# A transformer layer on one core: the first norm one section further ahead, the residual's input loaded a second time

## The chip, the core and the metric

The program runs on one core of one Trainium2 chip. A core has a matrix engine (TensorE, PE in the profile; its weight loads are PEld), a vector engine (VectorE, DVE), a scalar engine (ScalarE, ACT), a general engine (GpSimd, POOL) and a synchronising engine (SyncE, SP) that here issues nearly all DMA transfers. Each engine runs its own list of instructions in order, and they wait for each other on semaphores. The metric is the device time of one execution in microseconds, smaller is better.

## What is computed

One pre-norm layer on 4 sequences of 1024 tokens with 256 features: latent attention with 16 heads, then a mixture of 16 experts of which each token takes 2, beside a shared dense expert. Cut to what matters:

```python
h = layernorm(x)
q = (h @ Wqa @ Wqb)                      # 16 heads, 64 plain + 64 rotary columns
ckv, k_pe = split(h @ Wkva, 64)          # latent keys/values, rotary key
k, v = split(ckv @ Wkvb); rope(q_pe, k_pe)
x = x + softmax(causal(q @ k.T / sqrt(128))) @ v @ Wo     # the residual
h2 = layernorm(x)
top2 = top_k(softmax(h2 @ gate.T), 2)
out = x + sum_over_top2(w * swiglu(h2, expert)) + swiglu(h2, shared)
```

## The kernel before, in words

The 4096 tokens are 32 tiles of 128 rows. The program has a start (weights are multiplied together, scaled and split into pairs of 16-bit numbers), 32 attention sections with two more to drain them, then the experts' rows and the final sum. A batch is one sequence, 8 tiles, so 8 sections; section t is section t % 8 of its batch. A tile attends to all tiles before it in its batch, so sections grow: 2 units of heads in the first, 4 in the second, 8 in the third and fourth, 16 from the fifth on.

Section t does the attention of tile t, and beside it the side work of other tiles, at fixed places (unit k, place sub) from the tables `FIRST_TILE`, `SECOND`, `MIDDLE`, `LONG`, which all engines read. The side work, by tile:

- tile t+3: its first norm. VectorE makes mean and variance (`means`), GpSimd the rest (`norm`): 14 small steps for the inverse root, then xn, and the pair xs of 16-bit halves. SyncE turns xs into xT (`turn_x`), in one of two buffers.
- tile t+2: its projections by TensorE from xT into the one side bank of PSUM (`lat`, `pe0`, `pe1`, `q0`, `q1`). ScalarE and VectorE copy them out as high and low halves: the latent into `ks_sb`, the queries into `qs`, which lies in the tile `work` (`query_hi`, `query_lo`). Rotary columns go through GpSimd (`rope`). SyncE then turns the keys (`turn_keys`, ks_sb into kT) and the queries (`turn_queries`, work into qT). `query_hi` of a tile waits until the queries' transpose of the tile before has landed, since it overwrites what that one reads: `act.wait_ge(s.qT_in, 16 * n)`.
- tile t-1: the second half of the attention's output is normed, split and turned into oT (`turn_output`), TensorE multiplies it by the output weights (`out`), VectorE adds the input and writes x1 (`residual`). `means` and `norm` then take x1 of tile t-1 and the x of tile t+3 in one go, the x1 part first; SyncE turns both (`turn_x2`, `turn_x`).
- tile t-2: router and dense expert (`gate`, `up`, the hidden row turned by `turn_hidden`, `down`), and the rows are scattered to the experts' lists.

The input tiles stand in `x_sb`, five buffers, from the load until the residual has read them. So `load_x(m)` waits for the residual of tile m-5.

`section` of SyncE sets the order of all transposes, loads and stores in one queue, and a wait in it holds all that stands behind. `side` of TensorE puts the first projection that reads xT (`lat`) at (0, 3) in the second section of a batch, at (0, 1) in the third and fourth, at (0, 2) in the later ones.

## Time and profile before

| | us |
|---|---|
| runs (3), median | 1942.01 |
| lowest, highest | 1939.42, 1942.53 |
| profiled execution, its own time | 1940.04 |
| its span | 1938.2 |
| busy: PE, DVE, ACT, POOL | 1567.4, 1309.4, 1030.4, 978.7 |
| DMA moved | 139.76 MB, mean 72 GB/s |

The mean granted clock of TensorE is 0.924 of full speed. The span runs from the first instruction to the last end; the execution's own time has 1.8 us around it. An engine's busy time says how much it works, not whether the end waits for it. That is what the chain says: it is followed back from the last instruction, at each step to what released it. The list of waits counts every idle stretch that a wait ended, on the chain or off it.

### The profile page before, as it was taken

The page shows a single profiled execution, that of the slowest core. Times are in us where ns is not written, and L with a number is a line of the kernel's source. Part 1 is how long each engine was busy: PE and PEld are TensorE (multiplying, and loading weights), DVE is VectorE, ACT ScalarE, POOL GpSimd, SP SyncE. Part 2 cuts the span into 40 slices and gives each one's busy share as a digit, 9 for nine tenths or more (in the row PEclk, how much of TensorE's full clock was granted, in tenths as well). Part 3 has the DMA queues.
Part 4 walks back from the last instruction along what each step waited for, and adds up shares of the span by engine and source line. Part 5 has one row for each costly group of instructions (what it writes and reads, how often), then busy time and mean ns, then how long its engine had stood idle before and what let it go on. Part 6 is the DMA issues. An engine that isn't in the chain of part 4 may idle for free.

```text
span 1938.2 us, 45912 instructions
## 1 busy us (share of the span) xinstructions
PE 1567.4 (81%) x16418; PEld 1111.6 (57%) x16419; DVE 1309.4 (68%) x2960; ACT 1030.4 (53%) x2344; POOL 978.7 (50%) x1570
## 2 busy tenths in 40 slices
PE   8555779999868899997788999968889997379990
PEld 3133556766646667666466666655666765256660
DVE  1445877788766677887576787867667886245556
ACT  1323556666545666665455666645556663156660
POOL 2023656755566666644676664646566334134340
PEclk9667899999989999999899999989999999599995
DMA  5056333212234322213422323133322211543327
GB/s 151 0 153 120 55 60 71 60 31 46 58 63 88 65 57 53 44 25 59 93 60 56 56 56 54 30 67 72 64 55 50 51 23 31 124 138 104 102 81 260
DMA packets 329045, 139.76 MB, mean 72 GB/s; under 512 B 276656, under 2 KB 323795, under 8 KB 328790
## 3 DMA queue, kind: packets, MB, share of 16 engines
q1 hardware_dynamic: 313942, 113.14, 28.4%
q0 software_dynamic: 6912, 16.83, 2.7%
q10 hardware_dynamic: 8000, 7.23, 1.3%
q8 instruction: 123, 2.02, 0.4%
q14 instruction: 68, 0.56, 0.1%
HBM read 42.58 MB, written 29.53 MB: 37 GB/s over the span
## 4 chain that ended last, share of the span: by engine, by line
PE 50%; DVE 19%; ACT 7%; DMA 7%; issue 6%; POOL 6%; SPq 3%; DVEq 1%; ACTq 0%; POOLq 0%
PE of_ps L576 23%; PE s_ps L576 15%; PE t_ps L732 10%; DVE pT L1437 5%; DVE smax L1408 3%; ACT pT L885 2%; POOL xn L562 2%; DMA wd_sb<-wd 1%; ACT probs L1009 1%; DVE smax L1412 1%; DVE nmax L1416 1%; SPq L406 1%; ACT work L885 1%; DMA xT<-xs 1%; POOL xs L566 1%
## 5 line engine op out<-in xcount | busy, mean ns | idle before, releaser
L1437 DVE TENSOR_TENSOR pT<-t_ps,pT 128x512 f16<-128x512 f32 (+3 forms) x688 | 409.9, 598 | 188.7 <-ACT pT L885 186.6
L576 PE MATMUL s_ps<-kT,qT 128*128 128x512 f16 (+3 forms) x2304 | 498.9, 331 | 18.0 <-DMA qT<-work 14.1
L885 ACT CAST pT<-t_ps 128x512 f16<-128x512 f32 (+3 forms) x688 | 354.5, 515 | 271.4 <-PE t_ps L732 271.3
L732 PE MATMUL t_ps<-id,probs 128*128 128x128 f32 x2304 | 388.6, 284 | 67.6 <-ACT probs L1009 31.8
L732 PEld LDWEIGHTS t_ps<-id,probs 128*128 128x128 f32 x2304 | 262.6, 144 | 170.2 <-issue 84.8
L576 PE MATMUL of_ps<-weights,xT 128*128 128x512 f16 (+1 forms) x960 | 231.8, 385 | 136.6 <-DMA xT<-xs 87.7
L576 PEld LDWEIGHTS s_ps<-kT,qT 128*128 128x128 f16 x2304 | 221.0, 100 | 88.1 <-DMA qT<-work 14.3
L1009 ACT ACTIVATE probs<-s_ps,nmax,fac 128x640 f32<-128x640 f32 (+3 forms) x256 | 269.1, 1051 | 1.1 <-DVE nmax L1416 1.0
L576 PEld LDWEIGHTS of_ps<-ckv,pT 128*128 128x128 f16 x6912 | 244.4, 99 | 43.2 <-DVE o_sb L1278 10.4
L576 PE MATMUL of_ps<-ckv,pT 128*128 128x64 f16 x6912 | 261.2, 194 | 8.0 <-DVE o_sb L1278 7.7
L576 PEld LDWEIGHTS of_ps<-weights,xT 128*128 128x128 f16 x960 | 88.7, 108 | 230.6 <-issue 118.6
L1625 POOL TENSOR_TENSOR os_<-o_sb,os_ 128x512 f16<-128x512 f32 x64 | 74.7, 1167 | 224.6 <-ACT os_ L885 216.1
L1408 DVE TENSOR_REDUCE smax<-s_ps 128x1 f32<-128x512 f32 (+1 forms) x256 | 157.4, 648 | 3.9 <-PE s_ps L576 3.7
L1713 POOL DMA_INDIRECT y_exp<-probs,work x80 | 78.7, 984 | 149.3 <-ACT probs L1098 143.2
L1609 POOL TENSOR_TENSOR work<-work,sin_sb 128x544 f32<-128x544 f32 x64 | 102.0, 1594 | 96.8 <-ACT work L885 68.0
L885 ACT COPY work<-of_ps 128x512 f32<-128x512 f32 (+1 forms) x96 | 44.6, 464 | 199.3 <-PE of_ps L576 197.3
L1014 ACT ACTIVATE probs<-s_ps,nmax,fac 128x256 f32<-128x256 f32 (+3 forms) x224 | 144.1, 649 | 1.1 <-DVE nmax L1419 1.1
L1390 DVE TENSOR_REDUCE smax<-s_ps 128x1 f32<-128x768 f32 (+2 forms) x136 | 122.8, 903 | 13.0 <-PE s_ps L576 12.2
L576 PE MATMUL s_ps<-maskbf,idbf 128*128 128x128 bf16 x512 | 114.5, 224 | 0.0
L1412 DVE TENSOR_REDUCE smax<-s_ps 128x1 f32<-128x512 f32 (+2 forms) x160 | 95.4, 627 | 21.6 <-PE s_ps L576 21.3
L576 PE MATMUL of_ps<-weights,oT 128*128 128x256 f16 x768 | 90.7, 276 | 8.8 <-DMA oT<-os_ 6.0
L576 PEld LDWEIGHTS of_ps<-weights,oT 128*128 128x128 f16 x768 | 74.4, 99 | 21.6 <-ACT work L885 5.1
(201 smaller groups left out, 2448.5 us busy)
## 6 DMA issues: line engine op xcount, KB each, us to landing
work<-lists SPq DMA_DIRECT2D x80, 128.5 KB
wgu_sb<-wgu SPq DMA_DIRECT2D x2, 2816.0 KB, 14.9
x_sb<-x SPq DMA_DIRECT2D x32, 128.0 KB, 2.4
dense<-den SPq DMA_DIRECT2D x32, 128.0 KB
weights<-dense SPq DMA_DIRECT2D x1, 4096.0 KB, 17.9
qT<-y_exp SPq DMA_DIRECT2D x16, 256.0 KB, 5.8
work<-y_exp SPq DMA_DIRECT2D x16, 256.0 KB, 7.6
layer_out<-weights ACTq DMA_DIRECT2D x16, 256.0 KB, 5.7
```

Of the source, the lines that this page charges most:

```text
L576: return pe_.matmul(o, a, b, start=start, stop=stop)
L732: last = pe_.transpose(t_ps[:, h, c * P:(c + 1) * P], probs[:, u % 2, g * L + j * P:g * L + (j + 1) * P], id32[:, :])
L885: return act.copy(o, i)
L1009: act.activation(probs[:, par, 0:L], s_flat[:, 1024 * par:1024 * par + L], ACT.Exp, bias=nmax[:, par, 0:1], scale=f_att, accum_out=ssum[:, ...
L1014: last = act.activation(probs[:, par, g * L:(g + 1) * L], s_flat[:, base:base + L], ACT.Exp, bias=nmax[:, par, g:g + 1], scale=f_att, accu ...
L1390: dve.tensor_reduce(smax[:, par, 0:G], view, AX_X, ALU.max).then_inc(s.maxs, 1)
L1408: last = dve.tensor_reduce(smax[:, par, h:h + 1], bank[:, 0:(j1 - j0) * P], AX_X, ALU.max)
L1412: last = dve.tensor_reduce(smax[:, par, h * n:(h + 1) * n], view, AX_X, ALU.max)
L1437: dve.tensor_tensor(pT[:, u % 2, 1, h, 0:w], t_ps[:, h, 0:w], pT[:, u % 2, 0, h, 0:w], ALU.subtract).then_inc(s.lo_p, 1)
L1609: st_.do(pool.tensor_tensor(rot2[:, :, k:ROPE:2], pe[:, :, 1 - k:ROPE:2], sin_b, ALU.mult))
L1625: pool.tensor_tensor(os_[:, 1, :], o_sb[:, :], os_[:, 0, :], ALU.subtract).then_inc(s.lo_o, 1)
L1713: pool.indirect_dma_start(y_exp, bass.IndirectOffsetOnAxis(xg[:, q, 2 * D:ROW].bitcast(I32), 0), m_ys[:, q % YB, :], None, bounds_check=NY ...
```

## The change

The first norm is made one section further ahead: section t norms tile t+4 together with x1 of tile t-1. xT gets a third buffer, and so does `ks_sb`. The start makes three norms before the weights' scales instead of two. An input tile is done with once its norm is made, so `x_sb` has two buffers; for the residual the tile is loaded a second time (`load_residual`), straight into the x1 buffer in which the sum is then made in place. On SyncE, `load_x` now stands at the head of a section and waits for a norm of the section before; `load_residual` stands in front of the transpose of the second half of the attention's output.

```diff
--- before.py
+++ after.py
@@ -51,7 +51,8 @@
 UPRE = [sum(UNITS[:i]) for i in range(TB)]
 LN_STEPS = 14
 NEWTON = 3
-XS = 5
+XS = 2
+KS = 3
 SPLIT_MAX = [g > 1 or i >= 6 for i, g in enumerate(GROUP)]
 
 
@@ -184,13 +185,13 @@
         ln_w = sb("ln_w", [P, 3, 2], F32)
         xn = sb("xn", [P, D], F32)
         xs = sb("xs", [P, 2 * D], F16)
-        xT = sb("xT", [P, 2, 2, KD, P], F16)
+        xT = sb("xT", [P, 3, 2, KD, P], F16)
         NPE = (H + 1) * ROPE
         work = sb("work", [P, 2 * NPE + H * HD + HD], F32)
         pe = work[:, 0:NPE].rearrange("p (h r) -> p h r", r=ROPE)
         rot2 = work[:, NPE:2 * NPE].rearrange("p (h r) -> p h r", r=ROPE)
         qs = work[:, 2 * NPE:2 * NPE + H * HD].bitcast(F16).rearrange("p (s h d) -> p s h d", s=2, h=H)
-        ks_sb = sb("ks_sb", [P, 2, 2, HD], F16)
+        ks_sb = sb("ks_sb", [P, KS, 2, HD], F16)
         qT = sb("qT", [P, 2, 2, H * P], F16)
         kT = sb("kT", [P, 2, S], F16)
         ckv = sb("ckv", [P, 2, TB, C], F16)
@@ -245,7 +246,8 @@
         s = namedtuple("Signals", names)(*(sem(n) for n in names))
 
         xin = [sem(f"x_in{k}") for k in range(XS)]
-        k_in = [sem(f"keys_in{k}") for k in range(2)]
+        k_in = [sem(f"keys_in{k}") for k in range(KS)]
+        x1_in = [sem(f"x1_in{k}") for k in range(2)]
         xn_s = [sem(f"xn_made{k}") for k in range(2)]
         scattered = [sem(f"scattered{k}") for k in range(2)]
         stored = [sem(f"stored{k}") for k in range(2)]
@@ -337,7 +339,7 @@
         t_row, t_exp = t_tab[:, 0:1], t_tab[:, 1:2]
         tab = sb("tab", [1, 2, NMT], I32)
         free_i = sb("free_i", [1, E], I32)
-        pad = x_sb[:, 2:4, :].rearrange("p a n -> p (a n)").bitcast(F16)[:, 0:ROW]
+        pad = x_sb[:, 0:2, :].rearrange("p a n -> p (a n)").bitcast(F16)[:, 0:ROW]
         w_s, w_t = xn[:, 0:NT], xn[:, NT:2 * NT]
         w_k = xn[:, 2 * NT:4 * NT].rearrange("p (t k) -> p t k", k=TOPK)
 
@@ -366,7 +368,7 @@
             load(r_wqaT[0:QLB, 1, :], wqaT[P:QL, :], s.w_a)
             load(r_pe[:, 0, :], wqb_peT[0:P, :], s.w_a)
             load(r_pe[0:QLB, 1, :], wqb_peT[P:QL, :], s.w_a)
-            for k in range(3):
+            for k in range(XS):
                 load(x_sb[:, k, :], x[k * P:(k + 1) * P, :], xin[k])
             load(r_wvT, wvT, s.w_o)
             load(r_wo, wo.rearrange("(h d) n -> d h n", d=VD), s.w_o)
@@ -378,16 +380,21 @@
 
             def load_x(m):
 
-                if has(m - XS):
-                    sp.wait_ge(s.side_free, JOB["out", m - XS] + 1)
+                sp.wait_ge(s.ln1_done, 2 * (m - XS + 1))
                 sp.dma_start(x_sb[:, m % XS, :], x[m * P:(m + 1) * P, :]).then_inc(xin[m % XS], 16)
+
+            def load_residual(p):
+                if has(p - 2):
+
+                    sp.wait_ge(s.dense_done, p - 1)
+                sp.dma_start(x1[:, p % 2, :], x[p * P:(p + 1) * P, :]).then_inc(x1_in[p % 2], 16)
 
             def turn_x(m):
                 sp.wait_ge(s.ln1_done, 2 * (m + 1))
-                if has(m - 2):
-
-                    sp.wait_ge(s.side_made, JOB["q1", m - 2] + 1)
-                sp.dma_start_transpose(xT[:, m % 2].rearrange("p a k n -> p (a k) n"), xs[:, :]).then_inc(s.xT_in, 16)
+                if has(m - 3):
+
+                    sp.wait_ge(s.side_made, JOB["q1", m - 3] + 1)
+                sp.dma_start_transpose(xT[:, m % 3].rearrange("p a k n -> p (a k) n"), xs[:, :]).then_inc(s.xT_in, 16)
 
             def turn_x2(p):
                 sp.wait_ge(s.ln2_done, 2 * (p + 1))
@@ -413,7 +420,7 @@
 
                     last = n - i - 1
                     sp.wait_ge(s.s_made, 2 * (unit_of(last, units(last) - 1) + 1))
-                sp.dma_start_transpose(kT[:, :, i * P:(i + 1) * P], ks_sb[:, n % 2].rearrange("p s d -> p (s d)")).then_inc(k_in[n % 2], 16)
+                sp.dma_start_transpose(kT[:, :, i * P:(i + 1) * P], ks_sb[:, n % KS].rearrange("p s d -> p (s d)")).then_inc(k_in[n % KS], 16)
 
             def turn_output(p, hh):
                 sp.wait_ge(s.lo_o, 2 * p + hh + 1)
@@ -431,18 +438,19 @@
                                        hs[:, :, :].rearrange("p a n -> p (a n)")).then_inc(s.hT_in, 16)
 
             def section(t):
-                n, p, q, m = t + 2, t - 1, t - 2, t + 3
+                n, p, q, m = t + 2, t - 1, t - 2, t + 4
                 i = t % TB if has(t) else None
+                if has(m + 1):
+                    load_x(m + 1)
                 if has(q) and i == 0:
                     turn_hidden(q)
                 if has(p):
+                    load_residual(p)
                     turn_output(p, 1)
                 if has(q) and i not in (0, 1):
                     turn_hidden(q)
                 if i in (0, 2, 3):
                     turn_output(t, 0)
-                if has(m + 1):
-                    load_x(m + 1)
                 if has(p):
                     turn_x2(p)
                 if has(m):
@@ -463,7 +471,10 @@
                     store_dense(q)
 
             turn_x(0)
+            load_x(2)
             turn_x(1)
+            load_x(3)
+            turn_x(2)
             turn_keys(0)
             turn_queries(0)
             section(-1)
@@ -627,7 +638,7 @@
             def project(n, name, c0, w):
                 side_bank(name, n)
                 pe_.wait_ge(s.xT_in, 16 * (n + 1))
-                split_product(f_ps[:, 0:w], lambda a, k: xT[:, n % 2, a, k, :], lambda b, k: wq[:, b, k, c0:c0 + w],
+                split_product(f_ps[:, 0:w], lambda a, k: xT[:, n % 3, a, k, :], lambda b, k: wq[:, b, k, c0:c0 + w],
                               list(range(KD))).then_inc(s.side_made, 1)
 
             def latent(n):
@@ -696,7 +707,7 @@
                 G, par, L = GROUP[i], u % 2, (i + 1) * P
                 if u == 0 and h == 0:
                     pe_.wait_ge(s.qT_in, 16 * (t + 1))
-                    pe_.wait_ge(k_in[t % 2], 16 * (t // 2 + 1))
+                    pe_.wait_ge(k_in[t % KS], 16 * (t // KS + 1))
                 for g, j0, j1 in halves(i)[h]:
                     base = 1024 * par + s_off(i, g)
                     c0, c1 = j0 * P, j1 * P
@@ -926,11 +937,11 @@
                 if n > 0:
 
                     act.wait_ge(s.rope_done, n)
-                if n > 1:
-                    act.wait_ge(k_in[n % 2], 16 * (n // 2))
-                    act.wait_ge(s.ckv_ready, n - 1)
+                if n >= KS:
+                    act.wait_ge(k_in[n % KS], 16 * (n // KS))
+                    act.wait_ge(s.ckv_ready, n - KS + 1)
                 copy(pe[:, H, :], f_ps[:, C:2 * C])
-                copy(ks_sb[:, n % 2, 0, 0:C], f_ps[:, 0:C]).then_inc(s.hi_q, 1)
+                copy(ks_sb[:, n % KS, 0, 0:C], f_ps[:, 0:C]).then_inc(s.hi_q, 1)
 
             def rope_copy(n, g):
                 act.wait_ge(s.side_made, JOB[f"pe{g}", n] + 1)
...
@@ -1237,12 +1248,12 @@
 
             def latent_lo(n):
                 dve.wait_ge(s.hi_q, 3 * n + 1)
-                dve.tensor_tensor(ks_sb[:, n % 2, 1, 0:C], f_ps[:, 0:C], ks_sb[:, n % 2, 0, 0:C], ALU.subtract).then_inc(s.side_free, 1)
+                dve.tensor_tensor(ks_sb[:, n % KS, 1, 0:C], f_ps[:, 0:C], ks_sb[:, n % KS, 0, 0:C], ALU.subtract).then_inc(s.side_free, 1)
 
             def latent_copy(n):
 
                 dve.wait_ge(s.side_free, JOB["lat", n] + 1)
-                dve.scalar_tensor_tensor(ckv[:, :, n % TB, :], ks_sb[:, n % 2, :, 0:C], 1.0, ks_sb[:, n % 2, :, 0:C], ALU.mult,
+                dve.scalar_tensor_tensor(ckv[:, :, n % TB, :], ks_sb[:, n % KS, :, 0:C], 1.0, ks_sb[:, n % KS, :, 0:C], ALU.mult,
                                          ALU.max).then_inc(s.ckv_ready, 1)
...
@@ -1280,7 +1291,8 @@
 
             def residual(p):
                 dve.wait_ge(s.side_made, JOB["out", p] + 1)
-                dve.scalar_tensor_tensor(x1[:, p % 2, :], f_ps[:, 0:D], f_out, x_sb[:, p % XS, :],
+                dve.wait_ge(x1_in[p % 2], 16 * (p // 2 + 1))
+                dve.scalar_tensor_tensor(x1[:, p % 2, :], f_ps[:, 0:D], f_out, x1[:, p % 2, :],
                                          ALU.mult, ALU.add).then_inc(s.side_free, 1)
 
             def means(n, p):
@@ -1375,9 +1387,9 @@
                     out_norm(t, 0)
                 if due("out", p, t, k, sub):
                     residual(p)
-                    means(t + 3, p)
+                    means(t + 4, p)
                 if t == 0 and (k, sub) == (1, 3):
-                    means(3, -1)
+                    means(4, -1)
                 if due("down", q, t, k, sub):
                     places(q)
 
@@ -1446,6 +1458,7 @@
 
             means(0, -1)
             means(1, -1)
+            means(2, -1)
             first_weights()
             other_weights()
             latent_lo(0)
@@ -1455,7 +1468,7 @@
             rope_sum(0)
             rope_lo(0)
             lo_parts(FIRST, FIRST + 1)
-            means(2, -1)
+            means(3, -1)
             latent_lo(1)
             latent_copy(1)
             lo_parts(FIRST + 1, len(SPLITS))
...
@@ -1660,6 +1673,7 @@
 
             norm(pool, 0, -1)
             norm(pool, 1, -1)
+            norm(pool, 2, -1)
             pool.wait_ge(s.amax_ready, 1)
             pool.partition_all_reduce(amax_all[:, 0:2], amax[:, 0:2], P, bass.bass_isa.ReduceOp.max).then_inc(s.amax_reduced, 1)
             pool.wait_ge(s.amax_ready, 2)
@@ -1681,7 +1695,7 @@
                 if i in (0, 2, 3):
                     out_lo(t, 0)
                 if t < NT:
-                    norm(pool, t + 3, p)
+                    norm(pool, t + 4, p)
                 if i == 1:
                     if has(q):
                         hidden_lo(q)
```

SyncE's queue from the end of the first section of a batch (section 8) to the transposes of section 9, with the semaphores waited for. Before (lines: 416 keys, 406 queries, 377 dense store, 423 attention's output oT, 383 load of x, 397 and 390 the two norms, 430 hidden row):

```order
L416 DMA_TRANSPOSE kT<-ks_sb 128x2x128 [waits rope_done]
L406 DMA_TRANSPOSE qT<-work 128x32x128 [waits s_made,side_free,rope_done]
L377 DMA dense<-den 128x256 [waits dense_done]
L423 DMA_TRANSPOSE oT<-os_ 128x8x128 [waits side_made,lo_o]
L383 DMA x_sb<-x 128x256 [waits side_free]
L397 DMA_TRANSPOSE x2T<-xs 128x4x128 [waits side_made,ln2_done]
L390 DMA_TRANSPOSE xT<-xs 128x4x128 [waits side_made,ln1_done]
L430 DMA_TRANSPOSE hT<-hs 128x6x128 [waits side_made,lo_h]
L423 DMA_TRANSPOSE oT<-os_ 128x8x128 [waits side_made,lo_o]
```

and now (423 keys, 413 queries, 379 dense store, 384 load of x, 390 load of the residual's input, 430 oT, 404 and 397 the two norms, 437 hidden row):

```order
L423 DMA_TRANSPOSE kT<-ks_sb 128x2x128 [waits rope_done]
L413 DMA_TRANSPOSE qT<-work 128x32x128 [waits s_made,side_free,rope_done]
L379 DMA dense<-den 128x256 [waits dense_done]
L384 DMA x_sb<-x 128x256 [waits ln1_done]
L390 DMA x<-x 128x256 [waits dense_done]
L430 DMA_TRANSPOSE oT<-os_ 128x8x128 [waits side_made,lo_o]
L404 DMA_TRANSPOSE x2T<-xs 128x4x128 [waits side_made,ln2_done]
L397 DMA_TRANSPOSE xT<-xs 128x4x128 [waits side_made,ln1_done]
L437 DMA_TRANSPOSE hT<-hs 128x6x128 [waits side_made,lo_h]
L430 DMA_TRANSPOSE oT<-os_ 128x8x128 [waits side_made,lo_o]
```

The load of x has moved from behind oT to in front of it, and the new load stands there too.

SyncE's queue at the start, from the first transposed input to the first weights of the experts. Before:

```order
L390 DMA_TRANSPOSE xT<-xs 128x4x128 [waits ln1_done] x2
L416 DMA_TRANSPOSE kT<-ks_sb 128x2x128 [waits rope_done]
L406 DMA_TRANSPOSE qT<-work 128x32x128 [waits side_free,rope_done]
L383 DMA x_sb<-x 128x256
L390 DMA_TRANSPOSE xT<-xs 128x4x128 [waits side_made,ln1_done]
L416 DMA_TRANSPOSE kT<-ks_sb 128x2x128 [waits rope_done]
L406 DMA_TRANSPOSE qT<-work 128x32x128 [waits side_free,rope_done]
L360 DMA wgu_sb<-wgu 128x16x352 [waits lo_made]
```

and now:

```order
L397 DMA_TRANSPOSE xT<-xs 128x4x128 [waits ln1_done]
L384 DMA x_sb<-x 128x256 [waits ln1_done]
L397 DMA_TRANSPOSE xT<-xs 128x4x128 [waits ln1_done]
L384 DMA x_sb<-x 128x256 [waits ln1_done]
L397 DMA_TRANSPOSE xT<-xs 128x4x128 [waits ln1_done]
L423 DMA_TRANSPOSE kT<-ks_sb 128x2x128 [waits rope_done]
L413 DMA_TRANSPOSE qT<-work 128x32x128 [waits side_free,rope_done]
L384 DMA x_sb<-x 128x256 [waits ln1_done]
L397 DMA_TRANSPOSE xT<-xs 128x4x128 [waits side_made,ln1_done]
L423 DMA_TRANSPOSE kT<-ks_sb 128x2x128 [waits rope_done]
L413 DMA_TRANSPOSE qT<-work 128x32x128 [waits side_free,rope_done]
```

Each load of x now waits for a norm, a third xT stands ahead of the first keys, and the fourth (tile 3) ahead of the second keys; behind it the experts' weights come as before.

## Rows read from the trace of the kernel before

**Rows 1.** The page, part 4: shares of the chain that ended last, by engine.
```profile
...
PE 50%; DVE 19%; ACT 7%; DMA 7%; issue 6%; POOL 6%; SPq 3%; DVEq 1%; ACTq 0%; POOLq 0%
...
```

**Rows 2.** The list of waits: us in total, times, longest us.
```profile
...
PE of_ps L576 <- DMA xT<-xs: 87.7, 13, 18.5
...
```

**Rows 3.** TensorE in order of time: start, us, instruction [idle before <-releaser].
```profile
...
171.49 0.80 PE L576 MATMUL of_ps<-weights,xT 128*128 128x128 f16 x6 [18.52 <-DMA xT<-xs]
173.58 1.09 PE L732 MATMUL t_ps<-id,probs 128*128 128x128 f32 x4 [1.30 <-DVE pT L1437]
...
552.41 0.80 PE L576 MATMUL of_ps<-weights,xT 128*128 128x128 f16 x6 [9.96 <-DMA xT<-xs]
...
623.19 0.80 PE L576 MATMUL of_ps<-weights,xT 128*128 128x128 f16 x6 [4.87 <-DMA xT<-xs]
...
665.10 0.80 PE L576 MATMUL of_ps<-weights,xT 128*128 128x128 f16 x6 [4.67 <-DMA xT<-xs]
...
```

**Rows 4.** The chain in order of time, 545 to 590 us: start, us, what.
```profile
...
552.43 6.14 SPq L406
...
558.63 0.58 SPq L377
...
559.30 3.21 DMA oT<-os_
...
578.39 2.80 DMA hT<-hs
...
```

**Rows 5.** SyncE in order of time, a plain load of x.
```profile
...
541.13 0.58 SPq L383 DMA_DIRECT2D x_sb<-x  x1
```

**Rows 6.** Stretches: us, busy (x) of PE, PEld, DVE, ACT, POOL, then granted clock.
```profile
...
552.00:556.00 4.00, 3.59 (x20) 2.80 (x21) 1.32 (x4) 1.30 (x4) 1.96 (x3) 0.50 0.87 87
623.00:627.00 4.00, 3.81 (x19) 2.43 (x20) 1.82 (x5) 1.57 (x5) 1.46 (x2) 0.60 0.88 170
665.00:669.00 4.00, 3.90 (x35) 2.66 (x36) 1.41 (x4) 0.33 (x2) 1.38 (x2) 0.50 0.98 102
...
```

**Rows 7.** TensorE in order of time: out and down projections, sections 9, 32.
```profile
...
562.65 2.78 PE L576 MATMUL of_ps<-weights,oT 128*128 128x256 f16 x24 [1.35 <-DMA oT<-os_]
...
581.24 1.54 PE L576 MATMUL of_ps<-weights,hT 128*128 128x256 f16 x9 [1.49 <-DMA hT<-hs]
...
1635.85 4.45 PE L576 MATMUL of_ps<-weights,oT 128*128 128x256 f16 x24 [2.23 <-DMA oT<-os_]
...
```

**Rows 8.** The chain in order of time, 600 to 672 us.
```profile
...
620.63 2.42 DMA xT<-xs
...
662.55 2.41 DMA xT<-xs
...
```

**Rows 9.** SyncE in order of time: queries' transposes in sections 11, 12, 27.
```profile
...
623.21 5.22 SPq L406 DMA_TRANSPOSE qT<-work  x1
...
665.14 6.22 SPq L406 DMA_TRANSPOSE qT<-work  x1
...
1374.14 6.13 SPq L406 DMA_TRANSPOSE qT<-work  x1
...
```

**Rows 10.** DMA issues, the same three: median us from issue to landing.
```profile
...
qT<-work SPq DMA_TRANSPOSE x1, 7.7
...
qT<-work SPq DMA_TRANSPOSE x1, 7.9
...
qT<-work SPq DMA_TRANSPOSE x1, 8.9
```

**Rows 11.** ScalarE in order of time: first queries' copy, the same sections.
```profile
...
633.35 0.58 ACT L885 CAST work<-of_ps 128x512 f16<-128x512 f32 x1 [0.74 <-PE of_ps L576]
...
676.16 0.59 ACT L885 CAST work<-of_ps 128x512 f16<-128x512 f32 x1 [0.60 <-PE of_ps L576]
...
1384.29 0.59 ACT L885 CAST work<-of_ps 128x512 f16<-128x512 f32 x1 [0.74 <-PE of_ps L576]
...
```

**Rows 12.** GpSimd in order of time, 19 to 90 us.
```profile
...
59.44 0.38 POOL L1664 PARTITION_ALL_REDUCE amax_all<-amax  x1 [26.83 <-DVEq L1188]
...
```

More of the change, by code:

```diff
@@ L1501, in _ @@
             residual(NT - 1)
-            means(NT + 3, NT - 1)
+            means(NT + 4, NT - 1)
             places(NT - 2)
-            norm(dve, NT + 3, NT - 1)
+            norm(dve, NT + 4, NT - 1)
             gate_hidden(NT - 1)
```

8 lines of the change are left out of this document (4 added, 4 removed).

## The prediction

> **What bounds the kernel now.** I read the chain that ended last first. Half of it is TensorE, a fifth VectorE, and only 7% DMA and 6% GpSimd [rows 1]. The change goes after one wait. The list of waits says that TensorE's projections stood 13 times for the transposed input xT, 87.7 us in all [rows 2]. That is 4.5% of the span, and the first thing to settle is how much of it the end of the kernel feels. So I went to TensorE's own rows for each of the 13. They repeat by batch of eight sections: about 10.0 us in the second section of a batch, 4.9 and 4.7 in the fourth and fifth [rows 3]. The first batch has its own pair besides, 18.5 us in section 1 and a short one in section 2. By kind: one of 18.5, three of 10.0 (sections 9, 17, 25), eight of 4.4 to 4.9 (sections 3, 4, 11, 12, 19, 20, 27, 28), one short. For each kind I asked the chain whether it runs through that wait, and then what TensorE meets next once it is gone.
>
> **The change part by part.** The norm of tile t+4 instead of t+3 is made in section t. GpSimd makes as many norms, of the same size, at the same places; its order and its durations per section stay. xT of a tile is then needed a whole section later, 40 to 60 us, so all 13 waits should go. What each is worth:
>
> *Section 1, 18.5 us.* After this wait TensorE does 0.8 us of projection and stands again, for VectorE, until 173.58 [rows 3]. VectorE is held there by the search over the expert weights, whose load is issued from the same queue as before. TensorE will only reach 173.58 earlier. Worth 0. The short one in section 2 is followed in the same way by a wait for VectorE; I price it at 0.
>
> *Sections 9, 17, 25, 10.0 us each.* The chain does not run through this wait. It runs along SyncE's queue: keys, then the queries' transpose that takes the queue 6.14 us, the dense store, the transpose of the attention's output (oT) with 3.21 us to its landing, and then the out projection [rows 4]. That projection feeds the residual, the norm, the transpose of the hidden row and the down projection that closes the section [rows 4]. TensorE ahead of time meets oT at the same 562.5 and just waits longer before the out projection. The gain is 0. There is a cost. Two loads (the next x, and the new one of the residual) now stand between the dense store and this oT, where before there was none. One such issue is 0.58 us of SyncE [rows 5], two 1.2. Their 256 KB also go ahead of oT: between 0 and 1 us more, I take 0.3. And TensorE, with its earlier work (about 7 us at full clock) done 10 us sooner, stands some 12 to 14 us before the out projection instead of 1.35, and begins it at half clock. After the 10 us idle of before it ran at 0.50 [rows 6]. The same 24 matmuls took 4.45 us where the clock was low and 2.78 here [rows 7]: 1.7 us more, on the chain. Sum 3.2. Against it, the later chain leaves TensorE less idle before the down projection, which in the old trace starts slow (1.54 us for 9 matmuls) [rows 7]; I give back 0.3. So 2.9 per section, from 1.2 (issues alone) to 5, and 3 x 2.9 = 8.7 us lost.
> The Trainium skill, "DMA: Bandwidth & Descriptors", section "Queues, rings and completion order", says that SyncE's transfers share its own row of rings and that each DMA engine takes their descriptors in ring order. It speaks against the change at this place: by it the data of the two loads precede oT's, which is the upper end for that term (1 instead of 0.3); the trace shows the chain along this queue but no plain load ahead of an oT.
>
> *The eight waits of 4.4 to 4.9 us.* Here the chain does run through the wait, with the landing of xT 2.4 us after its issue [rows 8]. What is next late? ScalarE's copy of the query projection into the staging tile first waits until the transpose of the tile before has landed, since that transpose reads the same tile. That transpose is issued right behind xT: at 623.21, 7.7 us to its landing, so 630.9; the copy ran at 633.35. In section 12: 665.14 + 7.9 = 673.0, copy at 676.16. In section 27: 1374.14 + 8.9 = 1383.0, copy at 1384.29 [rows 9 to 11]. So the copy can move forward by 2.4, 3.1 and 1.3 us and no more. The other five, read the same way, average 2.7; all eight together 20 us. What stands queued behind this copy on ScalarE are the exponentials of the next unit and the copies of the turned probabilities, and TensorE waits for these. TensorE without the xT wait would be ready 4.9 us earlier, and 1.6 us more because the slow clock after that wait (0.60 over 4 us, in section 12 0.50) [rows 6] is gone too. So it arrives 6.5 us early and stands about 4 us for ScalarE. Such a stand may lower the clock again: a stand of 4.7 to 4.9 us did, one of 1.35 did not [rows 3, 6, 7]. If it does, 4 us at half speed cost about 2. I take 0.9 as the mean over the eight, 7 in all. Net of this part 20 - 7 = 13 us, from 20 - 16 = 4 to 20.
> The Trainium skill, "TensorE: Matmul & The Clock Gate", Part 1, says that idle is the low state and that activity releases it. By it the new stands, if long enough, are each paid twice, which is the lower end (4).
>
> *The rest.* The residual's reload is 32 more loads of 128 KB, 4 MB on 139.8. In all sections but those three SyncE has a free stretch for them, since it waits for GpSimd's next output. The wait that the residual gains is on a load issued before oT on the same queue, which is in long before the out projection ends. Third buffers for xT and keys remove dependences that the new order would create, and cost nothing. At the start one more norm, some 6 us of GpSimd, goes into 26.8 us in which GpSimd only waits for the first weights' maxima [rows 12]. VectorE waits for the norm before it, while the matmuls of the weights set the pace. Price 0; if that cover failed, 6 us once.
>
> **Sum.** 0 + 0 - 8.7 + 13 = 4.4 us faster. The profiled execution took 1940.0 us (span 1938.2), so 1935.6 by its own clock. It lies 2 us under the median of the runs, 1942.0, and inside their spread (1939.4 to 1942.5). From the median it is 1937.6. I predict 1937.5. A measurement of this kernel can tell about 0.2% (3.9 us) from no change.
>
> **Rivals.**
> 1. *All comes back.* If ScalarE's copy were not held by the queries, each of the eight would give its wait and the slow clock, 6.5 to 7.5, together 56 us, less 8.7: 1895; with everything in the list of waits 1854. For it: the chain's own rows with xT. Against it: the landings of the queries, 1.3 to 3.1 us under the copies [rows 9 to 11], and the chain of section 9 [rows 4]. Short of that, half of the excess could return where the staging wait is softer than I think: about 1915. Chance 0.15.
> 2. *Slower: SyncE's queue.* The mechanism is the one of sections 9, 17 and 25: two loads ahead of oT, then the out projection at half clock. At its upper price, 5 us, it costs 15; with the clock falling after each of the eight new stands their net is 4, so 1942 + 11 = 1953. It decides from the point where the eight give less than 3 x the loss, that is below 1.1 us each at my middle price of 2.9. For it: the chain along SyncE's rows, and a clock at 0.50 after each long idle. Against it: the copies may move 20 us. Chance 0.25.
> 3. *Nothing.* The same two, about equal (7 to 11 us each way): within 3.9 us of before, 1942. The change does what it says, and the waits only change their names. Chance 0.20.
>
> **How the numbers follow.** My forecast, small gain of 1 to 12 us (1930 to 1941), has 0.40; of that 0.28 lies beyond 0.2% and 0.12 within. Faster: 0.28 + 0.15 = 0.43. Same: 0.12 + 0.20 = 0.32. Slower: 0.25. The likeliest case's own range is 1930 to 1941. For 8 in 10 I reach into rival 1 to 1918, and into rival 2 to 1951.
>
> **What would show it.** In the new profile the wait of the projections for xT is gone or under 5 us. In its place: ScalarE's copies of the queries ended by the DMA of the queries, about 4 us in each of the eight sections; and TensorE's out projection in the second section of batches 2 to 4 ended by oT, some 12 to 14 us each, with a granted clock near 0.5 when it begins. If the copies of the queries do not wait, rival 1 holds. If the out projection of section 9 starts no later behind the issue of the queries' transpose than before (562.65 - 552.43 = 10.2 us), my loss term is wrong. A start of the first attention section later than before would contradict the free norm at the start.

## The result, and the profile after

The changed kernel takes 1943.2 us (median of 17 runs, 1940.8 to 1952.2) against 1939.5 us for the kernel before (17 runs on the same chip, 1935.5 to 1943.8). The ratio is 1.0029, with a 95% interval from 1.0017 to 1.0040: slower by 3.3 to 7.8 us (the two medians lie 3.7 us apart). I had predicted 1937.5 us, a small gain. The profiled execution took 1942.9 us, with a span of 1941.1 us. It lies 2.9 us over that of before.

The wait that the change was made for is gone. In the list of waits of the changed kernel, where the projections' wait for xT stood [rows 2], there are now these two (us in total, times, longest):
```profile
...
PE of_ps L587 <- DMA oT<-os_: 44.8, 4, 14.3
...
ACT work L896 <- DMA qT<-work: 36.2, 9, 6.4
...
```
The chain that ended last has less TensorE and more DMA and issue in it than before [rows 1]:
```profile
...
PE 44%; DVE 19%; DMA 9%; issue 8%; ACT 8%; POOL 7%; SPq 4%; DVEq 1%; ACTq 0%; POOLq 0%
...
```

To see where the time went I took the start of each tile's residual on VectorE from both traces, 32 marks, and subtracted. Sections are numbered as in the prediction; the residual of tile p stands in section p+1. Each line is the change of that difference over the sections named (worked out from the traces, plus is later):
```
start, sections 1 and 2                            -4.1
sections 3, 4                                      -6.2
section 5                                          +5.0
section 9 / 17 / 25                                +3.4 / +3.0 / +2.8
sections 11, 12 / 19, 20 / 27, 28                  -0.2 / -1.9 / -0.4
all other sections together                        +1.2
sum, at the residual of the last tile              +2.6
```

**Section 9.** The chain of the changed kernel in order of time (start, us, what), to be read beside [rows 4]:
```profile
...
547.14 5.20 SPq L413
...
552.39 1.05 SPq L379
...
553.49 0.43 SPq L384
...
553.97 0.46 SPq L390
...
554.53 3.59 DMA oT<-os_
...
558.25 5.29 PE of_ps L587 x24
...
```
and TensorE there, with the stretch of these 24 matmuls (us, busy of PE, PEld, DVE, ACT, POOL, then the granted clock):
```profile
...
558.25 5.28 PE L587 MATMUL of_ps<-weights,oT 128*128 128x256 f16 x24 [14.27 <-DMA oT<-os_]
...
```
```profile
...
558.00:563.20 5.20, 4.95 (x24) 3.45 (x25) 0.00 (x0) 0.00 (x0) 0.00 (x0) 0.50 0.00 0
...
```
The two plain loads (L384, L390) stand ahead of oT, TensorE has stood 14.3 us, and the projection takes 5.3 us at a clock of 0.50 (the lower level, 1.2 GHz) where it took 2.8 [rows 7]. Over the three sections, oT is issued 7.4 us behind the queries' transpose instead of 6.5 (means of three), and the projection takes 5.0 us instead of 2.8. That is 0.9 + 2.2 = 3.1 us, the mean of the three shifts. From oT's issue to the projection's start it takes 3.65 us on average, before 3.67, so against the kernel before no third term is needed.

**Section 11.** ScalarE's first query copy, TensorE behind it, and the issues of SyncE, each in order of time:
```profile
...
631.55 0.58 ACT L896 CAST work<-of_ps 128x512 f16<-128x512 f32 x1 [6.45 <-DMA qT<-work]
...
638.06 0.58 ACT L896 CAST work<-of_ps 128x512 f16<-128x512 f32 x1 [3.36 <-PE of_ps L587]
...
```
```profile
...
632.96 1.12 PE L743 MATMUL t_ps<-id,probs 128*128 128x128 f32 x4 [5.28 <-ACT probs L1025]
...
635.26 2.77 PE L587 MATMUL of_ps<-weights,xT 128*128 128x512 f16 x6
...
```
```profile
...
622.21 6.22 SPq L413 DMA_TRANSPOSE qT<-work  x1
...
```
```profile
...
qT<-work SPq DMA_TRANSPOSE x1, 9.0
...
```
This is the wait that was predicted in xT's place: the copy stands 6.45 us for the queries' landing, TensorE stands 5.28 us for ScalarE, and then runs slowly (6 matmuls of 512 columns in 2.77 us, where the same six take 1.46 at full clock in the trace of e2 below; the clock from 634 to 638 us is 0.50). What was not foreseen is the landing itself: 9.0 us after the issue, not 7.7 [rows 10]. The second copy comes 6.5 us behind the first, before 4.3. So section 11 became 1.9 us longer, not shorter. In section 12 (landing 7.8 us) the copy ran 20.9 us behind the residual of section 11 (673.87), before 24.1 (676.16 [rows 11]), and the section gained 2.2 us.

**Section 5.** GpSimd on the chain (start, us, what), and TensorE behind it, first in the changed kernel and then before:
```profile
...
284.65 5.83 issue
290.48 0.37 POOL amax_all L1715
...
290.93 6.88 issue
297.81 1.15 POOL os_ L1638
...
313.43 4.48 DMA hT<-hs
...
```
```profile
...
317.95 1.93 PE L587 MATMUL of_ps<-weights,hT 128*128 128x256 f16 x9 [3.35 <-DMA hT<-hs]
...
```
```profile
...
324.71 1.14 PE L576 MATMUL of_ps<-weights,hT 128*128 128x256 f16 x9
...
```
GpSimd's one reduction over the partitions for the expert weights blocks it for 13 us, as it did before. TensorE comes out of sections 3 and 4 ahead of time and now waits here for the hidden row, which GpSimd makes 2.7 us later behind the residual than before. Its landing is longer too, 4.5 us instead of 2.8. The down projection starts 11.4 us behind the residual instead of 7.9. In this trace that took 5.0 of the 6.2 us back. How much it takes differs from trace to trace: e4 and e1 below, the first with the same instructions up to here, landed this row in 2.8 us, waited 1.1 and 0.5 us for it, and lost 1.1 and 0.5 us in section 5; e8 landed it in 4.4 us and lost 5.2. Why the landing differs is not shown.

### The profile page after: what moved, and what is told of

Its sections match the earlier page's. It is cut to its first block, busy times and chain, and to the rows that moved or that the text cites. A ratio compares the mean times of both kernels' runs of the same rounds, so it can differ in the third digit from the quotient of the medians.

```text
span 1941.1 us, 45991 instructions
## 1 busy us (share of the span) xinstructions
PE 1561.6 (80%) x16418; PEld 1107.8 (57%) x16419; DVE 1310.0 (67%) x2960; ACT 1028.7 (53%) x2344; POOL 981.1 (51%) x1584
## 4 chain that ended last, share of the span: by engine, by line
PE 44%; DVE 19%; DMA 9%; issue 8%; ACT 8%; POOL 7%; SPq 4%; DVEq 1%; ACTq 0%; POOLq 0%
PE of_ps L587 20%; PE s_ps L587 13%; PE t_ps L743 9%; DVE pT L1449 5%; DMA qT<-work 3%; DVE smax L1420 3%; ACT pT L896 3%; POOL xn L573 2%; DMA wd_sb<-wd 1%; ACT probs L1020 1%; ACT probs L1025 1%; DVE nmax L1428 1%; DVE smax L1424 1%; ACT work L896 1%; SPq L413 1%
## 5 line engine op out<-in xcount | busy, mean ns | idle before, releaser
L587 PE MATMUL of_ps<-weights,xT 128*128 128x512 f16 (+1 forms) x960 | 218.7, 367 | 73.4 <-DVE ks_sb L1251 37.4
L587 PEld LDWEIGHTS of_ps<-weights,xT 128*128 128x128 f16 x960 | 83.7, 102 | 161.7 <-DVE ks_sb L1251 40.8
L587 PE MATMUL of_ps<-weights,oT 128*128 128x256 f16 x768 | 98.0, 289 | 47.6 <-DMA oT<-os_ 44.8
```

Of the source, the lines that this page charges most:

```text
L587: return pe_.matmul(o, a, b, start=start, stop=stop)
```

## Experiments

Each kernel was timed against the kernel before on the same chip; ratios have 95% intervals. "Shift" is the change of a section's length against the kernel before, from the traces. The runs of e1 to e4, e9 and e11 to e13 were made where the kernel before takes 1931 us, 0.4% less than here; in their traces the long sections (6 to 8, 13 to 16 and so on) are 0.3 to 1.1 us shorter for that reason, sections 3 to 5, 11 and 12 and their like in later batches by 0.2 at most, as those of e3 show, in which nothing was changed there; sections 9, 17 and 25 have no unchanged counterpart in these runs.

**Loads behind the output's transpose (e1).**
```
                 if has(p):
-                    load_residual(p)
                     turn_output(p, 1)
+                    load_residual(p)
+                if has(m + 1):
+                    load_x(m + 1)      # was first in the section
```


> The changed kernel with SyncE's two plain loads (next x, residual) issued behind the transpose of the attention's output instead of ahead of it, in every section. Theory (part of what sections 9, 17 and 25 lost is the place of the two loads in SyncE's queue): that transpose is issued 1.1 us earlier there, the out projection begins 1.1 to 1.5 us earlier, and the shift of the residual in these three sections against the kernel before falls from 3.4, 3.0 and 2.9 us to about 1.7; the out projection still runs at half clock. Time 1943.2 - 3 x 1.4 = 1939. Rival A (the whole loss is the clock after a stand of 14 us): the shift stays at 2.9 to 3.4, time 1943. Rival B (the loads' 256 KB cost wherever they stand, since they share the DMA engines): the issue moves but the landing does not, time 1943.

Measured 0.9999 (0.9984 to 1.0014), 0.30% below the changed kernel. SyncE in section 9:
```profile
...
547.69 5.20 SPq L413 DMA_TRANSPOSE qT<-work  x1
552.95 1.02 SPq L379 DMA_DIRECT2D dense<-den  x1
554.05 1.23 SPq L430 DMA_TRANSPOSE oT<-os_  x1
555.34 0.57 SPq L390 DMA_DIRECT2D x<-x  x1
...
```
Shifts 1.6, 1.6, 1.9 as the theory had it. oT is issued 1.0 us earlier behind the queries, and its data arrive 0.4 us sooner after the issue (3.2 against 3.65 us to the projection's start). The projection stays slow (5.0 to 5.3 us). Rival A falls by the shifts, rival B by the data's arrival. The ratio stands for 5.8 us, more than the three sections' 4.2; in this trace section 5 also lost less, so the ratio alone would not price the edit.

**Filler in the stand (e4).**
```
                 side_bank("out", p)
+                if p % TB == 0 and p > 0:
+                    for _ in range(60):
+                        mm(f_ps[:, 0:512], wq[:, 0, 0, 0:P], wq[:, 0, 0, 0:512], True, True)
                 pe_.wait_ge(s.oT_in, 32 * (p + 1))
```


> The changed kernel with 60 matmuls of 128x512 on constant weights into the free bank ahead of the wait for the output's transpose in the second section of batches 2 to 4, 12.8 us of work in a stand of 14.2 us; their result is overwritten. Theory (after the long stand the out projection runs at half clock, 5.3 instead of 2.8 us for 24 matmuls, on the chain): the granted clock stays at 1.0, the out projection takes 2.8 us, time 1943.2 - 3 x 2.5 = 1935.7. Rival A (the slow projection is not on the chain, or what follows absorbs it): matmuls faster, time 1942 to 1943. Rival B (the clock is not kept by such work, or falls elsewhere for it): no faster projection, time 1943 or more.

Measured 1.0009 (0.9997 to 1.0021). The projection of section 9:
```profile
...
555.39 2.79 PE L587 MATMUL of_ps<-weights,oT 128*128 128x256 f16 x24 [0.48 <-DMA oT<-os_]
...
```
All three run at 2.8 us; shifts 1.5, 1.2, 1.4. The clock is worth about 1.7 us each, a little less than the 2.2 of the matmuls. Both rivals fall by the projection's time and the shifts. By the times alone rival A would not: the interval overlaps that of the changed kernel (1.0017 to 1.0040), and the theory's 1935.7 us (0.998) lies below it.

**Both together (e15)**, with 56 matmuls of filler.

> The changed kernel with the loads behind the output's transpose, and 56 matmuls as filler in the stand of 12.8 us before the out projection of sections 9, 17 and 25; nothing done for the eight. Theory (the loss in these three sections is the queue's 1 us plus the clock's 2.2 us and nothing else): the residual's shift there goes from 3.4, 3.0 and 2.9 us to -0.2 to 0.3 against the kernel before; time against the kernel before 1.0029 - 9/1939 = 0.998. Rival (a third cause, as the residual's new wait on its reload, holds it once these two are gone): shift 1 or more, ratio 1.000.

Measured 0.9980 (0.9966 to 0.9994), and shifts of 0.0, 0.2 and 0.4 us. So the loss in sections 9, 17 and 25 is these two terms to within 0.4 us; the residual's wait on its reload is no third one.

**The norm back to tile t+3, reload kept (e3).**
```
-                n, p, q, m = t + 2, t - 1, t - 2, t + 4
+                n, p, q, m = t + 2, t - 1, t - 2, t + 3
-                    norm(pool, t + 4, p)
+                    norm(pool, t + 3, p)
```
The same goes for `means`, and the start makes two norms again.

> The changed kernel with the norm of tile t+3 in section t, as in the kernel before; the residual's reload, its two loads ahead of the output's transpose, two input buffers and three buffers for xT and keys stay. Theory: the 13 waits for xT come back with their old lengths (10.0 and 4.4 to 4.9 us), TensorE stands only some 2.5 us before the out projection of sections 9, 17 and 25 and runs it at full clock, so these lose only the issue term, 1.1 to 1.5 us each: 1939.5 + 4 = 1943.5, and the norm one section ahead is then worth nothing in sum (its gain in the eight is eaten by the clock in the three). Rival A (the reload costs nothing, the norm ahead all of the loss): 1939.5. Rival B (the reload costs more than the queue, by traffic or by the residual's new wait): 1946 or more.

Measured 1.0046 (1.0030 to 1.0062), which is rival B's size, though not by its mechanism. The 13 waits for xT were back (88.0 us). The out projection in section 9:
```profile
...
559.60 4.45 PE L585 MATMUL of_ps<-weights,oT 128*128 128x256 f16 x24 [2.88 <-DMA oT<-os_]
...
```
The loads make oT 1.0 to 1.3 us later, TensorE then stands 2.9, 3.8 and 2.4 us instead of 1.4, 1.5 and 0.9, and that is already enough: the projection takes 4.45, 5.28 and 4.45 us, shifts 2.7, 4.0, 2.8. My theory had full clock after such a stand. One microsecond of queue costs three. The norm ahead is not what loses the time, since with it (the changed kernel, 1.0029) the ratio is if anything lower; the intervals overlap. By these rows and by e1 the loads' place is; the norm back together with the loads behind oT was not run.

**The residual's load issued twice (e8)**, on top of e1, the second time into a spare tile.
```
+                sp.dma_start(spare[:, :], x[p * P:(p + 1) * P, :]).then_inc(spare_in, 16)
```


> The kernel with the loads behind the output's transpose, and each residual load issued twice, the second time into a spare tile that nothing reads: 32 more loads of 128 KB. Theory (a reload costs nothing by its traffic, only by its place ahead of the output's transpose): ratio as with the loads behind, 1.000 (0.9984 to 1.0014 measured). Rival (the traffic of the reload itself costs, by lengthening the landing of the transposes near it): 32 loads more cost what the first 32 did; if these were half of the changed kernel's loss, ratio 1.0015 or more.

Measured 1.0000 (0.9989 to 1.0011): 4 MB more cost nothing to be measured against e1 (0.9999), where about 0.2% could be told. The reload costs by its place, not its traffic.

**Queries first (e2).** SyncE's list of a section ends while TensorE is already in the next one: the queries that it issues last in its sections 10 and 11 are those that ScalarE's copy waits for in sections 11 and 12. So the edit is at i = 2 and 3.
```
                 if i in (0, 2, 3):
                     turn_output(t, 0)
+                if i in (2, 3) and has(n):
+                    turn_keys(n)
+                    turn_queries(n)
                 if has(p):
                     turn_x2(p)
...
-                if has(n):
+                if has(n) and i not in (2, 3):
```


> The changed kernel with the transposes of keys and queries issued ahead of those of x2 and x in the third and fourth section of a batch (i = 2, 3), where the queries stand ready while SyncE waits for GpSimd's norm. Theory (the eight waits for xT became ScalarE's wait for the landing of the queries' transpose, 6.5 and 4.0 us long, plus TensorE at half clock after its stand): the queries are issued about 10 us earlier, the wait of ScalarE's query copy in the eight sections goes, so does TensorE's stand of 5.3 and 2.9 us before the turns, and each gives 4 to 6 us: 1943.2 - 8 x 5 = 1903, at least 1915. Rival A (something else is as late there, as VectorE's low parts or GpSimd): the wait changes its name again, time 1938 to 1943. Rival B (the loss is all in sections 9, 17 and 25): 1943.

Measured 0.9828 (0.9811 to 0.9845): 39 us below the changed kernel. SyncE issues the queries 10 us earlier, while it would have waited for GpSimd's norm, and ScalarE's query copy in section 11 waits for TensorE alone:
```profile
...
608.14 1.89 SPq L423 DMA_TRANSPOSE kT<-ks_sb  x1
610.13 4.84 SPq L413 DMA_TRANSPOSE qT<-work  x1
615.06 1.23 SPq L404 DMA_TRANSPOSE x2T<-xs  x1
617.28 1.20 SPq L397 DMA_TRANSPOSE xT<-xs  x1
...
```
```profile
...
623.50 0.58 ACT L899 CAST work<-of_ps 128x512 f16<-128x512 f32 x1 [0.74 <-PE of_ps L590]
...
```
Sections 11, 12, 19, 20, 27 and 28 are each 6.2 to 6.5 us shorter than before, sections 3 and 4 together 7.4. The first rival of the prediction gave 6.5 to 7.5 each, 56 us for the eight, if the copy were not held; with it freed they give 45. Section 5 lost 4.7 us here too.

**The same order in the kernel before (e7).**

> The kernel before (norm of tile t+3, no reload, five input buffers) with keys and queries ahead of x2 and x in the third and fourth section of a batch. Theory (in the eight sections two things are late at the same place, xT at 13.0 us behind the residual and the landing of the queries at 20.6 to 21.9; removing either alone gives little): the query copy is free, but the projections still wait 4.7 to 4.9 us for xT, which follows GpSimd's norm; the copies stay at 23.2 and 24.1 us behind the residual. Ratio 0.999 to 1.001. Rival (the queries' landing alone was the limit, the norm ahead is not needed): 0.983.

Measured 1.0003 (0.9994 to 1.0011). TensorE in section 11:
```profile
...
622.43 0.80 PE L579 MATMUL of_ps<-weights,xT 128*128 128x128 f16 x6 [4.89 <-DMA xT<-xs]
...
```
Queries first alone: nothing. Norm ahead alone: nothing or a loss. Both: 1.7% below the kernel before. Two things were late at one place, and removing either only shows the other. This and e2 together are what shows the queries' landing as the limit of the eight sections.

**Filler ahead of the new stand (e9).**
```
                 # in turn(t, u, h)
+                if i == 3 and u == 2 and h == 1:
+                    pe_.wait_ge(s.lo_p, 2 * (g_ - 1) + h + 1)
+                    for _ in range(15):
+                        mm(t_ps[:, h, :], wq[:, 0, 0, 0:P], wq[:, 0, 0, 0:512], True, True)
                 pe_.wait_ge(s.exp_done, 2 * g_ + h + 1)
```


> The changed kernel with 15 matmuls of 128x512 on constant weights into the turn's own free bank, ahead of TensorE's wait for ScalarE's exponentials in the fourth section of each batch (sections 3, 11, 19, 27), where TensorE newly stands 3.7 to 5.3 us; 3.2 us of work, overwritten afterwards. Theory (the stand is paid twice there: after it TensorE runs at half clock, and the second query copy comes 5.8 to 6.5 us behind the first instead of 4.3): the distance of the two copies returns to about 4.3 us in sections 11, 19 and 27, each gains 1.5 to 2.2, 5 us in sum (section 3 stands elsewhere): ratio 1.0029 - 0.0025 = 1.0004. Rival (the distance of the copies is set by something else, or the clock falls all the same): 1.0029. If the fillers outlast the stand, each section loses their excess.

Measured 0.9992 (0.9981 to 1.0003). The query copies of section 19:
```profile
...
998.93 0.58 ACT L900 CAST work<-of_ps 128x512 f16<-128x512 f32 x1 [5.28 <-DMA qT<-work]
...
1003.03 0.59 ACT L900 CAST work<-of_ps 128x512 f16<-128x512 f32 x1 [1.02 <-PE of_ps L587]
...
```
4.1 us apart in sections 11, 19 and 27 instead of 5.8 to 6.5. The new stand was indeed paid twice. In section 3, where TensorE has no such stand, the same filler widened the distance from 4.1 to 7.2 us. Section 5 gained here too (its wait for the hidden row did not occur, since section 4 was slower in this run), so the 0.37% is not the filler's alone.

**The reduction later (e12).**
```
-                if t == 3:                      # behind the scatter
+                if t == 4:                      # behind the norm
                     pool.wait_ge(s.gu_amax, 1)
                     pool.partition_all_reduce(amax_all[:, 6:8], ...)
-                    if (t, k) == (4, 2):  expert_scales()
+                    if (t, k) == (4, 12): expert_scales()
```


> The changed kernel with GpSimd's one reduction over all partitions for the expert weights (14 us in which GpSimd does nothing else) moved from ahead of section 4's output part to behind section 4's norm, and VectorE's scales from it to a later unit. Theory (what sections 3 and 4 of the first batch gained, 6.2 us, was lost again in the next one because GpSimd, held by this reduction, had the hidden low part 2.6 us later against TensorE: its transpose landed at 11.3 us behind the residual, and the down projection waited 3.5 us): the residual of tile 4 keeps its 6 to 8 us lead, time 1943.2 - 5 = 1938, ratio 1.000. Rival (the 5 us are not GpSimd's but the transpose's own long landing, 4.5 us, or the reduction now holds something in the next section): ratio 1.002 to 1.004.

Measured 1.0038 (1.0021 to 1.0054). The wait for the hidden row went: the down projection started 7.9 us behind the residual instead of 11.4. But VectorE now stood 3.4 us for the reduction at its new place, and TensorE behind it:
```profile
...
331.68 1.09 PE L743 MATMUL t_ps<-id,probs 128*128 128x128 f32 x4 [4.40 <-DVE pT L1449]
...
```
Section 5 lost 6.1 us. So without GpSimd's lateness there is no such wait; that the 5 us can be had by a better place is not shown, and the rival is what came. The same edit on the candidate below (e13):

> The candidate with the later reduction as well. Theory: 5 us more, ratio 0.9735. Rival: with the reduction later GpSimd is late in the next section instead, ratio 0.976 or more.

Measured 0.9784 (0.9767 to 0.9800): the rival, and not to be told from the candidate without it (e11 below).

**Towards a faster kernel.** e5 is e1 and e2 together.

> The changed kernel with both edits: the two plain loads behind the output's transpose, and keys and queries ahead of x2 and x in the third and fourth section of a batch. Theory (two separate losses at different places): the gains add, 0.30% and 2.0% of the time before: ratio to the kernel before 0.9828 - 0.0030 = 0.980, 1900.5 us where before takes 1939.5. Rival (the loads behind the output's transpose now fall into the time in which the queries are in flight, and the one gain eats the other): ratio 0.983 or more.

Measured 0.9817 (0.9805 to 0.9830). The intervals of this and of e2 overlap, so additivity is not shown by the times; the shifts of sections 9, 17 and 25 are 1.6, 1.6 and 2.1 instead of 2.1, 2.9 and 2.7 in e2.

e10 adds:
```
                         turn_keys(n)
+                    if i == 0:
+                        turn_output(t, 1)       # and not again in the next section
                     turn_queries(n)
```


> The kernel with both edits, and in the first section of a batch the transpose of the attention's second output half (oT) issued between keys and queries instead of behind queries and dense store. Theory (in sections 9, 17 and 25 the chain is SyncE's queue: GpSimd has the output's low part ready 13.7 us before the residual in the changed kernel, and the queries' issue and the dense store stand ahead of oT): oT is issued 4 to 5 us earlier, the out projection starts that much earlier, 3 x 4.5 = 13 us: ratio 0.980 - 0.007 = 0.973. The queries go 4 us later there. Rival A (the later queries or the later dense store are then waited for, the gain is given back): ratio 0.979 to 0.982. Rival B (in the first batch, which has no SyncE queue in the way, the queries' delay costs and the others gain nothing): 0.983 or more.

Measured 0.9814 (0.9801 to 0.9827). Shifts of sections 9, 17, 25: -0.9, -1.1, -0.8, so 2.5 to 2.8 us better each than in e5. Sections 2 and 3 gave back 2.9 us: in the first batch the later queries are waited for (TensorE stood 3.0 us for them until 187.7). The 0.973 of the theory is missed, and rival A's size is what came. e11 leaves the first batch out of this edit and adds 36 matmuls of filler.

> Candidate: loads behind the output's transpose, keys and queries early in the third and fourth section, the output's transpose ahead of the queries' in the first section of batches 2 to 4 only (in the first batch it cost 2.8 us), and 36 matmuls of 128x512 as filler in the stand of 9.3 us before the out projection. Theory: from 0.9817 the transpose's place gives 3 x 2.5 = 7.5 us, the clock kept at 1.0 in the out projection another 3 x 1.2 = 3.6 (below the 2.2 of the projection itself, since VectorE's last wait there holds 0.9): ratio 0.9817 - 0.0057 = 0.976. Rival (VectorE or GpSimd sets the residual there, the filler gives nothing): 0.978.

Measured 0.9779 (0.9760 to 0.9799). The projection ran at full clock, but VectorE's residual did not follow it:
```profile
...
557.53 2.79 PE L593 MATMUL of_ps<-weights,oT 128*128 128x256 f16 x24
...
```
```profile
...
563.54 0.48 DVE L1304 SCALAR_TENSOR_TENSOR x<-of_ps,fac,x 128x256 f32<-128x256 f32 x1 [14.86 <-DMA x<-x]
...
```
Here the reload does hold the residual, by 3.2 us: it stands behind queries and dense store on SyncE's queue. e14 issues it right behind the output's transpose:

> The candidate (loads behind, queries early, output's transpose ahead of the queries' in batches 2 to 4, filler), and in the first section of batches 2 to 4 the residual's reload also ahead of the queries', right behind the output's transpose. Theory (with the output's transpose gone from the queue it is the reload that the residual waits for: the out projection ends 3.2 us before the residual, which starts 2.4 us after the reload's issue behind queries and dense store): the residual follows the projection by 0.04 us, 3 x 3.2 = 9.6 us: ratio 0.9779 - 0.005 = 0.973. Rival (GpSimd, which begins the queries' work then, or the queries 0.5 us later, takes it): 0.976 to 0.978.

Measured 0.9778 (0.9761 to 0.9795). The wait was gone (the residual at 557.21, projection 554.38 + 2.78), shifts -4.3, -4.5, -4.0; the next sections gave 3.6, 1.0 and 0.9 back. In the times that is not to be told from e11, as the rival had it. These two are the fastest kernels here, 2.2% under the kernel before.

## Why the prediction was wrong

*All 13 waits for xT go.* Right. *The start, section 1 and 2: worth 0.* Right as far as it can be told: the start is 4 us earlier in this trace, but see below.

*Sections 9, 17, 25: gain 0, cost 2.9 each.* Right in size, 3.1 each. Its terms: issues 0.9 (predicted 1.2) and clock 2.2 (1.7); the data's 0.3 had no row behind it and does not show against the kernel before (3.65 us from issue to start, before 3.67), though the way became 0.4 shorter when e1 took the loads away. The 0.3 that I gave back was not there: the down projection's 9 matmuls took 2.1, 2.1 and 1.9 us, before 1.5, 1.8 and 2.1 (they count in the shifts of sections 10, 18 and 26). The Trainium skill, "DMA: Bandwidth & Descriptors", section "Queues, rings and completion order", says that each DMA engine consumes the descriptors of a row of rings in ring order. From that I had set the upper end of this term, 1 us, by an estimate of mine. The trace agrees in sign, with the 0.4 us of e1.

*The eight waits: 20 us back, 7 lost to the clock, net 13.* This is the step that failed, in size. The name of the next wait (ScalarE's copy, for the queries' landing) and its place were right. In sections 11 to 28 the first copy moved forward by 0.8, 3.2, 2.2, 2.4, 2.2 and 1.6 us, 2.1 on average where I had 2.5. The step took the landings of before as fixed, and they were 7.6 to 9.2 us after the issue in both kernels, falling differently (9.0 instead of 7.7 in section 11, 9.2 instead of 7.6 in 28). Such a difference decides whether a section gains at all. Section 12 is 37.5 to 37.6 us long in the three traces with a landing of 7.6 to 7.8 us (the changed kernel, e1, e8), and 39.9 in the two with 9.1 and 9.3 (e4, e15), which is what it took before (39.7); e9 lies between, with 8.0 and 39.1. The clock after the new stand put 1.1 us on average between the two copies (predicted 0.9), and some more behind them (in section 12 it was 0.57 over the 4 us from 676, with the second copy at 676.75). In sum the six copies moved forward by 12.4 us where I had 15, the clock between the copies took 6.8 and the time behind them 3.0 where I had 5.4, and 2.6 us were left. Sections 3 and 4 gave 6.2, where I had 3.2. So net 8.7 instead of 13.

*What is late next, once more.* I asked it for the eight sections, but not for the one behind them. Section 5 took 5.0 us back through GpSimd. With this the eight are worth 3.7 us, less than half of the 9.3 that the three cost. The size is that of one trace: with the same order of the queries e8, e4 and e1 give 3.3, 4.9 and 5.7 us for the same nine sections, and e15 loses 1.0. None comes near 13. The second rival had the mechanism right (two loads ahead of oT, then half clock, and the eight's net too small); its deciding point, "below 1.1 us each", was met at 3.7 / 8 = 0.5. Beside the two steps, the sections that I had at nothing were 1.2 us longer in sum.

*The reload costs nothing, third buffers nothing.* Right for its traffic (e8) and for the residual's wait (e15). But its issue ahead of oT is the larger part of the loss by what it sets off: with the norm back, the loads alone cost 9 us (e3).

*The chance that the clock falls after a stand.* I had seen it fall after 4.7 us and not after 1.35. Stands of 2.4 and 2.9 us were enough (e3). The kernel before had shown as much: the third line of [rows 7], which I read for its 4.45 us alone, has a stand of 2.23 us ahead of it. The Trainium skill, "TensorE: Matmul & The Clock Gate", Part 1, has idle as the low state. The trace agrees: after 14.3 us of standing the projection of section 9 ran at 0.50 and took 5.3 us.

## What to carry to other kernels

When a wait is removed, ask at the same place for the second latest input, and then ask again one section on: here two waits of equal length covered each other, either edit alone gave nothing, and both gave 1.7%. On a queue that leads to a critical transfer, the place of a cheap load can count where its bytes don't: here 1 us of issue against 4 MB of traffic. A short delay in front of an idle TensorE is paid again in its clock, so 1 us of queue became 3 us of time (e3). And a landing time read once is one draw: here it differed by up to 1.7 us at the same place, where the forecast rested on a gain of 2.5.

## What the runs showed of the hardware

- The out projection (24 matmuls, 2.78 us) took 4.45 us after stands of 2.4 and 2.9 us (e3), 4.2 to 5.3 after longer ones, 2.8 after 0.9 to 1.7 us (the kernel before and e7), and 2.8 where matmuls on constants filled the stand to within 0.5 us. The length of the last stand alone does not decide: in the last section it took 4.2 to 5.3 us in every trace, after 1.35 to 2.3 us, and there TensorE had stood 1.8 us shortly before as well (in e1, one of the three with 1.35, the clock was at 0.50 already ahead of that stand).
- The queries' transpose (one issue of 4.7 to 6.6 us on SyncE) landed 6.6 to 9.8 us after its issue, and 7.6 to 9.3 us at the same place (section 27) in kernels with the same order there that differ elsewhere. What decides it stays open; a longer issue goes with it in section 11 (6.2 and 9.0), but not in 28 (5.2 and 9.2).
- The first issue of the queries' transpose in the program came at 93.6 to 93.8 us in three kernels and at 96.4 to 97.9 in all others, the kernel before among them, with the same instructions up to there in most. The 4 us that the changed kernel's trace gains at its start look to be of this kind (e9, the second of the three, has them too; in e5, the third, the first residual is only 0.7 us early, with an out projection of 4.4 us ahead of it), and are luck. Without them it would lie 6.7 us over the kernel before at the last residual, and the ratio of the runs stands for 5.6 (1939.5 x 0.0029).
